# Reordering the start, the batch-one normalisation and the router of a first attention on one Trainium2 core

## The reference

```python
mod = (_silu(L0_c) @ L0_wmod).reshape(L0_c.shape[0], 6, 1, -1)
sa, ca, ga, sb, cb, gb = ...          # ga, gb pushed away from zero
h = _layernorm(x, axis=-1) * (1 + ca) + sa
Q, K, V = h @ Wq.T + bq, h @ Wk.T + bk, h @ Wv.T + bv
x = x + ga * (softmax(causal(Q @ K.T / sqrt(128))) @ V)
h = _layernorm(x, axis=-1) * (1 + cb) + sb
# router: logits = h @ router_w.T, first maximum of 8 experts, place within the
# expert by a running count over all 2048 rows, capacity 384; y = the expert's MLP
x = x + gb * y
```

## Time and profile before

| | us |
|---|---|
| median of three runs | 973.53 (973.2 to 974.91) |
| the profiled execution's own time | 973.75 |
| its span | 972.0 |
| PE busy | 909.9 (94%) |
| DVE busy | 593.1 (61%) |
| ACT busy | 642.2 (66%) |
| POOL busy | 292.5 (30%) |

### The profile page before, as it was taken

How to read it: one execution, slowest core, us unless ns; L and a number is a source line. 1 busy time by engine, 2 the same in 40 slices (tenths; PEclk the granted TensorE clock), 3 DMA queues, 4 the chain that set the end, 5 groups by cost and what they waited for, 6 DMA issues and landing times. The chain is left out here.

```text
span 972.0 us, 25390 instructions
## 1 busy us (share of the span) xinstructions
PE 909.9 (94%) x10211; PEld 668.2 (69%) x10211; DVE 593.1 (61%) x1355; ACT 642.2 (66%) x1094; POOL 292.5 (30%) x367
## 2 busy tenths in 40 slices
PE   7998897369999999999999999999999999998987
PEld 6676576146777767777776777777677777776776
DVE  5556111566666666666666666666666666677975
ACT  2552143158787878778787878778787877884442
POOL 5124800503224242422324142232414223215110
PEclk9998799569999999999999999999999999999999
DMA  8300701100020002002000200100020010000000
GB/s 251 137 2 22 254 26 52 40 1 2 2 90 3 2 2 92 2 2 84 9 3 1 91 2 2 76 17 2 2 91 1 3 31 10 3 1 2 1 23 22
DMA packets 27128, 35.48 MB, mean 37 GB/s; under 512 B 6042, under 2 KB 21716, under 8 KB 26836
## 3 DMA queue, kind: packets, MB, share of 16 engines
q1 hardware_dynamic: 25988, 31.76, 10.0%
q0 software_dynamic: 1024, 2.10, 0.7%
HBM read 28.48 MB, written 5.37 MB: 35 GB/s over the span
## 5 line engine op out<-in xcount | busy, mean ns | idle before, releaser
L552 DVE CUSTOM_DVE_ANT_0 soft<-SC,strips 128x1024 f32<-128x1024 f32 x256 | 303.3, 1223 | 79.7 <-PE SC L394 79.6
L513 ACT ACTIVATE soft<-soft,nmax 128x1024 f32<-128x1024 f32 x256 | 294.1, 1150 | 3.5 <-DVE nmax L552 3.4
L430 PE MATMUL CX<-PTs,V 128*64 128x256 f32 x2048 | 244.7, 381 | 0.0
L498 ACT COPY PTs<-PT 128x1024 f32<-128x1024 f32 x128 | 129.6, 1013 | 139.2 <-PE PT L413 139.2
L394 PE MATMUL SC<-qk 64*128 64x512 f32 x1536 | 212.5, 409 | 7.0 <-DVE nmax L552 6.9
L413 PEld LDWEIGHTS PT<-ident,soft 64*128 64x128 f32 x4096 | 159.0, 139 | 70.2 <-issue 28.9
L430 PEld LDWEIGHTS CX<-PTs,V 128*64 128x64 f32 x2048 | 142.6, 137 | 92.8 <-issue 35.0
L560 DVE COPY PTs<-PT 128x512 f32<-128x512 f32 x128 | 88.5, 692 | 161.0 <-PE PT L413 161.0
L413 PE MATMUL PT<-ident,soft 64*128 64x64 f32 x4096 | 176.4, 226 | 3.9 <-ACT PTs L505 2.4
L394 PEld LDWEIGHTS SC<-qk 64*128 64x128 f32 x1536 | 137.8, 188 | 32.9 <-issue 5.2
L341 POOL CAST qk<-raw_qk 128x512 fp32r<-128x512 f32 x60 | 36.8, 614 | 262.3 <-ACT raw_qk L317 262.3
(11 more groups left out here) (268 smaller groups left out, 998.2 us busy)
## 6 DMA issues: line engine op xcount, KB each, us to landing
strips<-bias_vec SPq DMA_DIRECT2D x8, 1920.0 KB, 7.0
arena<-in_L_ffn_w SPq DMA_DIRECT2D x1, 2048.0 KB, 11.3
slots_in<-arena SPq DMA_DIRECT2D x1, 1536.0 KB, 9.3
arena<-slots_in SPq DMA_DIRECT2D x8, 192.0 KB, 4.5
slots_out<-arena SPq DMA_DIRECT2D x8, 192.0 KB, 2.0
x<-in_L_attn_x SPq DMA_DIRECT2D x2, 512.0 KB, 4.4
out<-x SPq DMA_DIRECT2D x4, 256.0 KB, 2.3
arena<-in_L_wmod SPq DMA_DIRECT2D x2, 384.0 KB, 4.8
```

Of the source, the lines that this page charges most:

```text
L430: ins = pe.matmul(CX[hd * DK:(hd + 1) * DK, 0:2 * P], V1[:, vb, t, hd * DK:(hd + 1) * DK], PTs[:, g % 2, hd, t, :], start=(t == 0), stop=( ...
L498: act.copy(turned_out(n, 0), turned_in(0)).then_inc(ev("ptA_out"), 1)
L513: act.activation(soft[:, n % RING, hd, :], soft[:, n % RING, hd, :], ACT.Exp, bias=nmax[:, j:j + 1], scale=-1.0, accum_out=rsum[:, hd, n % ...
L552: dve.tensor_tensor_reduce(soft[:, n % RING, hd, :], SC[hd][:, :], strips[:, u // B % 2, hd, i * P:i * P + S], 1.0, 3.4e38, ALU.add, ALU.m ...
```

## The change

- At the start: three dummies instead of six, none after the weights' transposes; `mod_rows` is split into `mod_columns` and `mod_vectors`, and the vectors are issued behind `turn_rows(0, 0)`. ACT scales the first half of batch zero before it copies the vectors, and the second half after. DVE copies the columns ahead of its rows.
- Fills are issued in the order 0, 1, 3, 4, then scores of tiles 0 and 1, then the v fills 2 and 5. Fill 2 has another bank. Batch one's rows, transposes and fills move behind tile 1's context. DVE writes batch one's rows after `biased0(1)`.
- Batch zero's inverse roots move from POOL to DVE, in step 11. `rows_out` goes to the start of step 12, ahead of `biased0(12)`; its transposes to step 12, into the banks PT, with a wait for `turned0(10)`; ACT's scaling to step 12; the logits to step 13, the ranks to step 15, `router_choice(0)` to step 14, `slot_places(0)` ahead of `added0(14)`.
- Behind the loop 26 dummies instead of 14.

```diff
@@ -230,9 +230,11 @@
         fills0 = [(kind, b, half) for b in range(B) for half in range(2) for kind in "qkv"]
-        fill_banks = [PT[0], PT[1], four_sc[0], CX[:, :], MI[:, :], four_sc[1],
+        fill_banks = [PT[0], PT[1], four_sc[3], CX[:, :], MI[:, :], four_sc[1],
                       PT[1], four_sc[1], four_sc[3], PT[1], four_sc[1], four_sc[3]]
         order0 = list(range(TB)) + list(range(NT - 1, TB - 1, -1))
...
+        issued0 = (0, 1, 3, 4, 2, 5, 6, 7, 8, 9, 10, 11)
@@ -291,7 +293,7 @@
             if n == 1:
-                return four_sc[(3, 1, 0, 2)[k]]
+                return (PT[0], PT[1], four_sc[0], four_sc[2])[k]
             return four_sc[k]
@@ -748,8 +750,6 @@
-            pool.wait_ge(ev("var_ready"), batches_until(1, 0))
-            inverse_roots(tiles(0))
             pool.wait_ge(ev("h_ready"), 6)
@@ -840,7 +840,7 @@
                         continue
-                    act.wait_ge(ev("proj0_full"), f + 1)
+                    act.wait_ge(ev("proj0_full"), issued0.index(f) + 1)
                     dst = (q0T if kind == "q" else k0T)[:, b * S + half * 512:b * S + half * 512 + 512]
@@ -864,20 +864,21 @@
+            norm_out(0, (0,), (0,))
             mod_out(0)
-            norm_out(0, (0,))
+            norm_out(0, (0,), (1,))
             act.wait_ge(ev("bq_scaled"), 1)
...
             for i in range(NT + 2):
+                if i == 4:
+                    turned0(2)
+                    norm_out(0, (1,))
+                    fills_out(1)
                 if i < NT:
                     exp0(i)
-                if i >= 2:
+                if 2 <= i != 4:
                     turned0(i - 2)
-                if i == 2:
-                    norm_out(0, (1,))
-                if i == 3:
-                    fills_out(1)
-                if i == 14:
+                if i == 12:
                     norm_out(1, (0,))
@@ -1032,7 +1033,7 @@
                 dve.wait_ge(ev("gate0_folded"), 1)
-                dve.wait_ge(ev("proj0_full"), f + 1)
+                dve.wait_ge(ev("proj0_full"), issued0.index(f) + 1)
                 tt(v0[:, t0:t0 + 4, :], fill_banks[f].rearrange("p (t d) -> p t d", d=D), bc_tiles(bvg[:, b, :], 4),
@@ -1066,14 +1067,12 @@
             inverse_roots(tiles(0))
+            mod_columns(0)
             rows_out(quarter(0), rows0)
-            mod_columns(0)
             rows_out(quarter(1), rows0)
...
             inverse_roots(tiles(1))
-            values0(2)
-            rows_out(tiles(1), rows0)
             dve.wait_ge(ev("consts"), 8)
@@ -1120,28 +1119,35 @@
             for i in range(NT):
+                if i == 12:
+                    rows_out(tiles(0), rows0)
+                if i == 4:
+                    added0(1)
+                    values0(8)
+                    values0(11)
                 biased0(i)
                 if i == 1:
+                    rows_out(tiles(1), rows0)
+                if i == 2:
+                    values0(2)
                     values0(5)
-                if i >= 3:
+                if 3 <= i != 4:
                     added0(i - 3)
-                if i == 3:
-                    values0(8)
-                    values0(11)
                 if 4 <= i != 11:
...
                     stats0(7)
-                if i == 12:
-                    dve.wait_ge(ev("inverse_ready"), 1)
-                    rows_out(tiles(0), rows0)
+                if i == 11:
+                    dve.wait_ge(ev("var_ready"), batches_until(1, 0))
+                    inverse_roots(tiles(0))
+                if i == 14:
+                    router_choice(0)
             stats0(NT - 4)
-            router_choice(0)
             added0(NT - 3)
             stats0(NT - 3)
+            slot_places(0)
             added0(NT - 2)
             stats0(NT - 2)
-            slot_places(0)
             added0(NT - 1)
@@ -1316,7 +1322,7 @@
                 if n == TILES - 3:
-                    dve.wait_ge(ev("inverse_ready"), 2)
+                    dve.wait_ge(ev("inverse_ready"), 1)
                     rows_out(tiles(0))
@@ -1367,27 +1373,28 @@
             pe.transpose(MI[:, 0:NROWS], rows[0:NROWS, :], ident[0:NROWS, 0:NROWS]).then_inc(ev("rows_turned"), 1)
-            keep_clock(PT[0], 6)
+            keep_clock(PT[0], 3)
             pe.wait_ge(ev("ld_w0"), 48)
...
             ins.then_inc(ev("w0_turned"), 1)
-            keep_clock(PT[0], 4)
...
-            def mod_rows(layer):
...
+            def mod_columns(layer):
...
                 ins.then_inc(ev("modc_full"), 1)
...
+            def mod_vectors(layer):
...
                 for b in range(B):
...
             pe.wait_ge(ev("ld_wmod"), 16)
-            mod_rows(0)
-            keep_clock(PT[0], 4)
+            mod_columns(0)
@@ -1397,9 +1404,10 @@
+            keep_clock(PT[0], 4)
             pe.wait_ge(ev("w0T_ready"), 1)
             turn_rows(0, 0)
-            keep_clock(PT[0], 2)
+            mod_vectors(0)
             turn_rows(0, 1)
@@ -1407,6 +1415,8 @@
                 pe.wait_ge(ev("hT_ready"), 2 * b + half + 1)
+                if f == 2:
+                    pe.wait_ge(ev("mod_copied"), 2)
                 if f == 8:
@@ -1429,8 +1439,6 @@
                     pe.wait_ge(ev("qk0_out"), 2)
-                if i == 1:
-                    pe.wait_ge(ev("v0_out"), 1)
                 if i >= 2:
@@ -1449,6 +1457,8 @@
                     pe.wait_ge(ev("pt0_out"), j)
+                if j == 11:
+                    pe.wait_ge(ev("hT_ready"), 6)
                 for t in range(width0(j) // P):
@@ -1458,6 +1468,7 @@
                     pe.wait_ge(ev("qk0_out"), j + 3)
+                    pe.wait_ge(ev("v0_out"), 1)
                 else:
@@ -1497,32 +1508,35 @@
-            for f in range(5):
+            for f in (0, 1, 3, 4):
                 fill(f)
             for i in range(NT + 3):
+                if i == 4:
+                    turn0(2)
+                    context0(1)
+                    pe.wait_ge(ev("v0_out"), 2)
+                    turn_rows(0, 2)
+                    turn_rows(0, 3)
+                    for f in range(6, 12):
+                        fill(f)
                 if i < NT:
...
                 if i == 1:
+                    fill(2)
                     fill(5)
-                if 2 <= i < NT + 2:
+                if 2 <= i < NT + 2 and i != 4:
                     turn0(i - 2)
-                if i >= 3:
+                if 3 <= i != 4:
                     context0(i - 3)
-                if i == 2:
-                    pe.wait_ge(ev("v0_out"), 2)
-                    turn_rows(0, 2)
-                    turn_rows(0, 3)
-                if i == 3:
-                    for f in range(6, 12):
-                        fill(f)
-                if i == 13:
+                if i == 12:
+                    pe.wait_ge(ev("pt0_out"), 11)
                     turn_rows(1, 0)
                     turn_rows(1, 1)
+                if i == 13:
+                    logits0(0)
                 if i == 15:
-                    logits0(0)
-                if i == 17:
                     ranks0(0)
-            keep_clock(PT[0], 14)
+            keep_clock(PT[0], 26)
             turn_rows(1, 2)
@@ -1543,7 +1557,8 @@
             pe.wait_ge(ev("logits_shifted"), 2)
-            mod_rows(1)
+            mod_columns(1)
+            mod_vectors(1)
             pe.wait_ge(ev("vec_ready"), 1)
```

## The result

The changed kernel takes 984.78 us (median, 981.78 to 988.16) where the kernel before took 974.15 beside it: a ratio of 1.0113, interval 1.0088 to 1.0137. It is slower by 10.6 us; 3.2 were forecast. The profiled execution took 981.78 us (span 980.0), which is 8.0 more than the profiled one of before (span 972.0); these 8.0 us are what the rows can explain.

The account below looks back on a forecast made before the run. The chain through batch one's slot numbers, scatters and slots' load to the experts' start was taken as the bound; -0.5 + 4.1 + 1.0 + 1.1 - 2.5 = +3.2 us on 973.53 gave 976.7 us, range 973.0 to 979.6.

Parts of the forecast that it names:

- Part 1: Start up to scores0(4): it begins 0.6 us later, but tile 2's transposes and tile 1's context are already done; -0.5 us.
- rival (a): PE's clock holds in both new standstills, of 2.5 and 4.1 us: +0.8 us in sum, 974.3 us; chance 0.25.
- Part 2: Tile 12: batch zero's roots and rows on DVE delay biased0(12), so PE stands still waiting for turned0(10); +4.1 us.
- Part 3: Behind tile 12's standstill: PE restarts at half clock for some 2.7 to 3.4 us; +1.0 us.
- Part 4: Batch zero's router, scores0(13) to last variance: PE waits 0.9 us for hot rows, 1.5 us before turn0(14); +1.1 us.
- Part 5: Behind the loop: 26 dummies keep full clock through batch one's transposes and logits, 4.5 us to DVE's first reduction; -2.5 us.
- Rival (c): Dummies behind the loop don't hold the clock, or delay the transposes: no gain there, sum +5.7, 979.2 us; chance 0.13.
- One answer, 0 taken: Experts' start behind the second scatter: PE's 3.89 us wait may grow and cost clock; 0 taken, up to +1.7 us.

Follow-up runs that it names:

- e8_after14: The changed kernel with 14 dummies behind the loop instead of 26: 980.10 us, ratio 1.0067 to the kernel before.
- group 4: Side by side on one chip: kernel before (968.3 us), changed kernel (1.0058), kernel before with 26 dummies (0.9980), kernel before with bias table products and load earlier (0.9923).
- group 1: Kernel before with one part each: 26 dummies 1.0004, start 1.0001, batch zero's placement 1.0051; also changed kernel with 15 dummies in tile 12's wait, 1.0103.

## Why the prediction was wrong

- **Part 1** (-0.5): +0.4 in the profile, nothing in the time of the start alone. The term that was off is the pair of modulation vectors, taken at 2.0 us: with fewer dummies in front they took 3.32. The gate and fill 2 came 2.1 us later than the walk has them (24.17 against 22.05). That the sum is off by 0.9 only is luck: the fills behind were priced at half clock and ran at full clock, as rival (a) has it.
- **Part 2** (+4.1): right, 3.9 (scores0(13)'s place in PE's queue at 72.01 against 67.70, less the 0.4 of the start). Every link of the chain and the 3.73 us of idle time are in the rows. The root operations took 0.17 us each and 0.20 from one to the next, on to rows_out at 67.68. The Trainium skill, page "VectorE: DVE Perf Modes", section on the TRN2 errata, whose 58 cycles made the eleven 0.76 us by estimate, does not agree with that row; its measured fixed term of about 150 cycles does.
- **Part 3** (+1.0): mis-sized. Right is +2.2 (2.1 with the gap filled, 2.2 with the wait shortened, 1.9 where the clock did not fall). I took the 3.4 us of half clock from the standstills of before; here it lasted 6.8, as in five of the six profiles of kernels with this start and this gap of 3.7 us; in the sixth (e8_after14) it did not come at all, as rival (a) has it, and in batch zero's placement alone it lasted 3.4. What decides between the three is not shown.
- **Part 4** (+1.1): right in sum as far as a remainder can tell, 7.7 - 0.4 - 3.9 - 2.2 = 1.2, with both waits at their places (0.73 of 0.9, 1.39 of 1.5).
- **Part 5** (-2.5): this step failed, and it is the larger part of the miss: 0 (10.39 us from the transposes to the slot numbers, 10.44 before). The step is "the way from the transposes to the first reduction shrinks to 4.5 us", with logits of 3.41 us that the full clock was to bring down to 1.89. But 3.41 us is the time from the logits' start to DVE's reading (91.38 to 94.79); the logits' own row has 1.95, since the clock had come back just before them (0.68 from 90 to 91 in the earlier trace rows). So the full clock had only the transposes to win, 1.1 us (2.56 us to the logits' start in the dummies alone, 3.69 before), and the 1.46 us behind the logits' end was a wait of another kind that was there to be asked about: nothing on DVE or PE accounts for it, and batch zero's reading stands 0.04 us behind its logits (75.53 + 1.85 and 77.42). What the clock won was then lost: in the changed kernel ACT's second normalisation came 1.3 us after its transposes, the reading 0.95 us after the logits, and DVE waited 0.6 us for the ranks behind the table's products (0.16 before). With the dummies alone the reading came 2.74 us after the logits; had it come at once, the ranks would have held in its place, and by group 4 only 0.3 us would have been won. Rival (c) had the value, by other mechanisms than the true one: the clock held, and the transposes were not delayed. Where the execution with 14 dummies has the half clock through its logits, the term was near: at 968 the dummies alone gave 2.0 us at the slot numbers (97.48 against 99.49) and 2.2 in the time.
- **One answer, 0 taken**: the experts' start came 8.7 us later and the slot numbers 7.6; the slots' load took 5.17 us for all eight and not 4.21.

So in the profile 0.4 + 3.9 + 2.2 + 1.2 + 0 = 7.7, and 8.0 with what lies behind. The median of 984.78 is 3 us above the profiled execution and above the second median of the same program (981.47), and no run explains these 3 us; repeated, the ratio was 1.0085 and 1.0113 where the logits are held and 1.0058 where not. The change also loses more where they are held: ACT's second normalisation comes 1.3 us after its transposes there (96.94 to 98.24), and after 0.16 us of idle time, at 96.55, in the other level's profile. That was read from profiles and not tested alone. Where the logits are not held the change costs 5.2 us, and the forecast of +3.2 is short by 2.0.

## What to carry to other kernels

Before crediting a gain to an earlier producer, subtract its end from the consumer's start in the trace of before: a remainder that no queue explains (here 1.46 us) is a wait for something else, and a faster producer does not shorten it. Check too that the producer's own row has the length that the gain is worked out from. An operation of 2 us that is put ahead of the one link every other engine waits for costs its length and the half clock behind the gap; the same operation one place later cost under half. And look for the large transfer that shares the DMA engines with the last small one of the critical chain: moving its issue, and the products that make it, 14 us earlier was worth more than all placements of this change.

## What the runs showed of the hardware

- Signals from TensorE arrived late at VectorE while indirect DMAs of GpSimd were out, in some groups and not in others on the same chips: the same wait was 2.74 us (group 1) and 0.04 us (group 4) for the same program, and 0.04 us at the level of 974 with no scatter out. What sets the state is open.
- The last scatter's data were there 2.3 us after its issue with the DMA engines free (five profiles), and 5.0 to 7.0 us after it where a load of 3.84 MB had been issued 1 to 5 us before it (fifteen profiles).
- A standstill of 3.7 us on TensorE was followed by 6.8 us at 1.2 GHz in five profiles, by 3.4 us in one and by none in one (e8_after14); a wait of 1.70 us left it at 2.4 GHz.
